# Layer-0 cross attention: which operand of the probabilities-times-context product is stationary

## The chip, the cores and the metric

The kernel runs on one core of a Trainium2 chip. The metric is device time in microseconds (us), from launch to end of one execution. Three timed runs of the kernel before gave 3319.53, 3310.01 and 3318.12 us, median 3318.12. The profile is of a further execution. Its span, from first to last instruction, is 3369.6 us, 1.6% above that median; profiling makes it longer. A difference read in the profile is therefore multiplied by 3318/3370 = 0.985 before it is set against the runs.

## The reference, cut to what matters

A two-layer Perceiver block on 128 sequences of 32 tokens with 256 features. Each sequence has its own context of 257 rows with 256 features. The part that is changed is the first residual term:

```
x = x + L0_xattn(layernorm(x), ctx)
q = x1 @ Wq + bq ; k = ctx @ Wk + bk ; v = ctx @ Wv + bv
attn = softmax(q k^T / sqrt(256))           # 32 x 257 for each sequence, one head
out  = attn @ v                             # 32 x 256
```

Then follow self attention (16 heads), a quantised feed-forward network (FFN), cross attention with 16 heads on the same context (layer 1), self attention, and a mixture of experts. Everything is computed in float32 or in pairs of float16 numbers. Since the rows of attn sum to one, out = (attn @ ctx) @ Wv + bv. The kernel uses that: it forms attn @ ctx (called a1) and multiplies it by Wv afterwards.

## The kernel before, in words

A tile is four sequences, 128 tokens on 128 partitions; there are 32 tiles. Three parts run after each other: the first (layer-0 attention, self attention, FFN and the layer-1 cross attention), the second, and the third (experts). This change touches the first part and the seam to the second.

The first part runs two lanes, each with its own buffers and its own four banks of PSUM (`ps[:, 0..3]`). A tile is split in a first half of steps (`tensor1`, `scalar1`, `vector1`: from the norm of x to the FFN's two up products) and a second half (`tensor2`, `scalar2`, `vector2`: the FFN's last product and the layer-1 cross attention). While one lane is in the second half of its tile (the older lane, `o`), the other is in the first half of the next tile (the younger, `y`). One such overlay is called a half period here; there are 31 of them in the first part, and the younger lane's product a1 stands in each once. Together with the first tile, which runs alone, that makes 32 products.

Each engine is an in-order queue. In which order an engine takes the steps of both lanes is written out by hand as a string of `o` and `y` in `ORDER["first"]` (one string for each engine, and one for SyncE, which issues the loads). `ORDER["between"]` holds the same for the seam, which runs once. A wait in one step holds up everything behind it on that engine. Steps announce their end on a semaphore that `did(name)` counts, and `need(name)` waits for it. `STEPS` lists the names for each engine.

The steps around the change, in the younger lane: `s1_ps` (scores of four sequences, each on its own 32 columns of TensorE), `exps1` (exponential on ScalarE), `pt1_ps` (three transposes, L557), `pt1_f` (ScalarE copies them to SBUF as `pt1`), `a1_ps` (L565 and L569), `a1_f` (ScalarE copy to `op`), `y1_ps` (times Wv, L401), and `x_1` (VectorE adds the result to x, L923), followed by the next norm (`xn2`, L892) and its transposes (`xt_ps2`, L528).

The product a1 is formed turned, features on partitions and tokens on columns, as `y1_ps` needs it. For each of the two halves of the features there is one 128x128 product for the last context row of each sequence (L565: context stationary), and eight products for four sequences by two groups of 128 context rows (L569). In each of these the context (128 rows x 128 features) is the stationary operand and 32 columns of turned probabilities are the moving one. A float32 product shows in the trace as two MATMUL records with a weight load each.

The older lane meanwhile forms values (`v4_ps`, L381, 128x256), the last value row (`vl_ps`, L651, one 32-column group of TensorE for each sequence), and keys (`k4_ps`, L381, 128x257). VectorE copies the keys (`k4_f`, L1004) and ScalarE copies `vl` four times with a scale (`vl_f`, L843). Then come eight score products (`s4_ps`, L682) and eight rounds of turned scores (`st4_ps`, L711 and L715) and values (`o4_ps`, L732 and L735). Between the rounds VectorE takes a reciprocal (L1014) and multiplies (L1015, `om4`), which frees the bank for the turned scores two rounds on. At the end are `sel` (L1020), `y4_ps` (L781) and `x_4` (L1024). The half period ends when VectorE has the quantised activations `hq` (L984) and TensorE turns them (`hq_ps`, L742).

Of the kernel before, what the change touches and what calls it, by code (L numbers as in the profile page):

```python
# [13 lines left out]
P = 128  # L14
D = 256
C = D // P
SEQ = 32
SEQS = 128
KEYS = 257
NB = P // SEQ  # L20
# [79 lines left out]
def each(names, n):  # L100
# [3 lines left out]

STEPS = {
    "xattn": dict(
        tensor="xt_ps1 q0_ps qbk_ps s1_ps pt1_ps a1_ps y1_ps".split(),
        scalar="xt1_f q0_hi q0_hi exps1 pt1_f a1_f".split(),
        vector="ln_var1 xn1 q0_lo q0_lo exp_bias1 p1_last x_1".split(),
        gpsimd="ln_rstd1 biased1".split()),  # L110
    "selfattn": dict(
        tensor="xt_ps2 qk_ps v_ps self_s self_pt o2_ps self_y".split(),
        scalar="xt2_f qe_act v2_f self_p pt2_f sel2_act sel2_act".split(),
        vector="ln_var2 xn2 qk_f qe self_shift p2_norm sel2 sel2".split(),
        gpsimd="ln_rstd2 biased2".split()),
    "ffn": dict(
        tensor="xq_ps gate_ps gate_ps up_ps up_ps".split(),
# [5 lines left out]
        scalar=["hqt"]),  # L123
# [35 lines left out]
for _stage, _engines in STEPS.items():  # L159
    for _engine, _names in _engines.items():  # L160
# [12 lines left out]

ORDER = {
    "first": dict(
        tensor=("oyoyoyyooooyooyoyooooyoyooyooooyoooyoyooyooooooyyooyyooyoo"),
        scalar=("oyyyoooyoyooooooyooyoooyyoyooyoyyoooooyoyyooo"),
        vector=("yyyyoyoooooyyoyyyoyyooooyyoyyyoyoooyooooyooyyyyyooyyooyyyyoyoyyyooyyyyooyyooyyooyooyoyyyyyo"),
        gpsimd=("yoyyoooyoyo"),
        sync=("yyyyyyyyooo"),  # L180
    ),
    "between": dict(
        tensor=("oooyooooooooooooooooooooooyooyyooyyyyooyyooyoooooo"),
        scalar=("oooooooooooooooooyyyooyoyooyoooyyoyyoyoyoyy"),
        vector=("oyyyyyooooooooooooooooooooooyyoyoyooyoyoyyoyoyyyyooooyooooooyy"),
        gpsimd=("yoooooo"),
        sync=("ooo"),
    ),
# [54 lines left out]
def carve(memory, at, words, dt=F32):  # L243
    a = memory[:, at:at + words]
    return a if dt == F32 else a.bitcast(dt)


def build(nc, x_in, ctx_t, ctx_n, ctx_l, weights, ffn, experts, expert_b, consts, biases, rows, mid, sorted_rows, pair_rows, out):
    ctx = ExitStack()
    with ctx:  # L250
# [47 lines left out]
        def w1(name, k, n):  # L298

            a = W1_AT + W_AT[0][name]  # L300
            return mem[:, a:a + k * n].rearrange("p (k n) -> p k n", k=k)
# [96 lines left out]
        def by_token(pe, dst, weight, act, k=C):  # L398

            for kc in range(k):  # L400
                last = pe.matmul(dst, act[:, kc], weight[:, kc], start=(kc == 0), stop=(kc == k - 1))  # L401
            return last


        def first_half(lane):
# [15 lines left out]

            probs = carve(arena, 2048, KEYS)
            pt1 = carve(arena, 2308, 384)

            qe = carve(arena, 0, 512).rearrange("p (c b e q) -> p c b e q", c=C, b=NB, e=2)
            s2 = carve(arena, 512, 512)
# [106 lines left out]
            def tensor1(pe, t):  # L533
                def need(name, n=1):
                    pe.wait_ge(*at(t, name, n))
# [24 lines left out]
                need("pt1_f")  # L560
                pe.wait_ge(s[f"l_in{lane}"], total(t, 16, 16))
                pe.wait_ge(s[f"n_in{lane}"], total(t, 64, 64))
                for c in range(C):
                    cols = slice(c * P, (c + 1) * P)
                    pe.matmul(ps[:, 2, cols], ctx_lf[:, cols], pt1[:, 256:384], start=True, stop=False)  # L565
                    for b in range(NB):
                        for m in range(2):
                            toks = slice(m * P + SEQ * b, m * P + SEQ * (b + 1))
                            last = pe.matmul(ps[:, 2, c * P + SEQ * b:c * P + SEQ * (b + 1)], ctx_nf[:, b, m, cols], pt1[:, toks],  # L569
                                             start=False, stop=(b == NB - 1 and m == 1))  # L570
                last.then_inc(*did("a1_ps"))
                yield
                need("a1_f")
                by_token(pe, ps[:, 3, 0:D], w1("v0", C, D), op).then_inc(*did("y1_ps"))
                yield

# [22 lines left out]
                    last = pe.transpose(ps[:, 1, g * P:(g + 1) * P], s2[:, g * P:(g + 1) * P], ident)  # L599
                last.then_inc(*did("self_pt"))  # L600
                yield
                need("v2_f")
                need("pt2_f")
                pe.sem_inc(s["pe_goes"], 1)
                for c in range(C):
# [179 lines left out]
            def act_copy(act, t, dst, src, done, ready, n=1):  # L785

                act.wait_ge(*at(t, ready, n))
                act.activation(dst, src, ACT.Copy).then_inc(*did(done))  # L788
                yield

            def scalar1(act, t):
                yield from act_copy(act, t, xt[:, :, :].rearrange("p c n -> p (c n)"), ps[:, 0, 0:D], "xt1_f", "xt_ps1")
                act.wait_ge(*at(t, "q0_ps"))
                for c in range(C):
                    act.activation(q0[:, 0, c], ps[:, 1, c * P:(c + 1) * P], ACT.Identity, bias=qk_bias[:, c:c + 1]).then_inc(*did("q0_hi"))
                    yield
                act.wait_ge(*at(t, "exp_bias1"))
                act.activation(probs, ps[:, 0, 0:KEYS], ACT.Exp, bias=small[:, 3:4], accum_out=small[:, 4:5]).then_inc(*did("exps1"))
                yield
                yield from act_copy(act, t, pt1, ps[:, 1, 0:384], "pt1_f", "pt1_ps")  # L800
                yield from act_copy(act, t, op[:, :, :].rearrange("p c n -> p (c n)"), ps[:, 2, 0:D], "a1_f", "a1_ps")

                yield from act_copy(act, t, xt[:, :, :].rearrange("p c n -> p (c n)"), ps[:, 0, 0:D], "xt2_f", "xt_ps2")
                act.wait_ge(*at(t, "qk_f"))
                act.activation(qe[:, :, :, 0, :], qk_f[:, 0:2].rearrange("p c (b q) -> p c b q", b=NB), ACT.Copy, scale=parity[:, 0:1]).then_inc(*did("qe_act"))
                yield
                yield from act_copy(act, t, v2, ps[:, 0, 0:D], "v2_f", "v_ps")
                act.wait_ge(*at(t, "self_shift"))
                act.activation(s2, s2, ACT.Exp, scale=16 ** -0.5).then_inc(*did("self_p"))
                yield  # L810
                yield from act_copy(act, t, pt2.rearrange("p g n -> p (g n)"), ps[:, 1, :], "pt2_f", "self_pt")
                act.wait_ge(*at(t, "o2_ps"))
                for c in range(C):
                    act.activation(op[:, c].rearrange("p (b q) -> p b q", b=NB), ps[:, :, 64 * c:64 * c + SEQ], ACT.Identity,
                                   scale=parity[:, 0:1], bias=bcol("bv0")[:, c:c + 1]).then_inc(*did("sel2_act"))
                    yield

                yield from act_copy(act, t, xqt.rearrange("p c n -> p (c n)"), ps[:, 3, 0:P].bitcast(BF16), "xqt", "xq_ps")
                act.wait_ge(*at(t, "gate_ps", 1))
                act.activation(th3[:, 0:512], ps[:, 0, :], ACT.Tanh, scale=small[:, 11:12]).then_inc(*did("tanh"))  # L820
                yield
                act.wait_ge(*at(t, "gate_ps", 2))
                act.activation(th3[:, 512:1024], ps[:, 1, :], ACT.Tanh, scale=small[:, 11:12]).then_inc(*did("tanh"))
                yield
# [1116 lines left out]
```

## Time and profile before

| What | Value |
|---|---|
| median of three runs | 3318.12 us |
| span of the profiled execution | 3369.6 us |
| TensorE matmul (PE) busy | 2701.8 us, 80% |
| TensorE weight loads (PEld) busy | 2102.4 us, 62% |
| VectorE (DVE) busy | 1869.2 us, 55% |
| ScalarE (ACT) busy | 1046.4 us, 31% |
| GpSimd (POOL) busy | 495.2 us, 15% |
| mean granted TensorE clock | 0.913 |

Start with the shares of busy time, then look at the first part alone (62 to 2042 us), and there at one half period in order of time. Busy times of matmuls are modelled and overlap each other in latency. The distance between the starts of neighbouring rows is what a step costs TensorE, not the duration in the row. Granted clock 1.00 is 2.4 GHz and 0.50 is 1.2 GHz; a fraction between them is a mean over both.

### The profile page before, as it was taken

The numbers are of one execution on the slowest core, as the hardware profiler recorded it, in microseconds if no ns is written. First come the engines' busy times: TensorE is split into PE (matmuls) and PEld (weight loads), VectorE is DVE, ScalarE is ACT, GpSimd is POOL, SyncE is SP. The second block draws the span as 40 slices with busy tenths as digits, with TensorE's granted clock in tenths as the row PEclk, the third lists the DMA queues.
The fourth block names the chain that finished last, engine by engine and source line by source line (L and its number), as shares of the span: only waits on it lengthen the run. The fifth ranks groups of instructions, "written<-read, shape, count | busy, mean of one in ns | idle before, by whom it ended". The sixth has DMA issues, their size and how long they took to land.

```text
span 3369.6 us, 114292 instructions
## 1 busy us (share of the span) xinstructions
PE 2701.8 (80%) x45688; PEld 2102.4 (62%) x45783; DVE 1869.2 (55%) x5000; ACT 1046.4 (31%) x2120; POOL 495.2 (15%) x616
## 2 busy tenths in 40 slices
PE   3788888888888888888888887787788888858882
PEld 3566666676676676676676675566666666646662
DVE  4555556655655655655655655555555555545555
ACT  1333333333333333333333333222222222212220
POOL 2111111111111111111111111011111111112221
PEclk9889989988998998998999998899999999979996
DMA  5011111111111111111111112200000000021225
GB/s 176 22 38 50 30 38 51 30 41 48 31 43 44 32 42 44 32 43 44 32 43 43 33 45 72 96 14 17 14 14 14 16 14 14 14 73 62 69 66 178
DMA packets 86140, 153.57 MB, mean 46 GB/s; under 512 B 11224, under 2 KB 39904, under 8 KB 84576
## 3 DMA queue, kind: packets, MB, share of 16 engines
q1 hardware_dynamic: 73136, 117.78, 11.5%
q0 software_dynamic: 6528, 17.87, 1.4%
q10 hardware_dynamic: 6192, 13.38, 1.1%
q8 instruction: 270, 4.42, 0.5%
q14 instruction: 14, 0.11, 0.0%
HBM read 120.37 MB, written 28.62 MB: 44 GB/s over the span
## 4 chain that ended last, share of the span: by engine, by line
issue 54%; PE 24%; DVE 8%; POOL 6%; ACT 3%; DMA 2%; DVEq 2%; SPq 0%; POOLq 0%; ACTq 0%
PE ps L381 15%; POOL mem L463 3%; PE ps L1164 2%; PE ps L1479 2%; POOL x L1036 2%; PE ps L1116 1%; POOL rstd L1030 1%; DVEq L1457 1%; DVE mem L1348 1%; DVE mem L1527 1%; DMA y_tok<-mem 1%; DVE mem L1322 1%; DVE mem L1378 1%; DVE mem L1379 1%; DVE mem L1382 1%
## 5 line engine op out<-in xcount | busy, mean ns | idle before, releaser
L381 PE MATMUL ps<-mem 128*128 128x256 f16 (+1 forms) x4224 | 566.2, 293 | 76.1 <-DVE mem L1348 66.9
L381 PEld LDWEIGHTS ps<-mem 128*128 128x128 f16 x4224 | 439.2, 106 | 168.4 <-DVE mem L1348 70.4
L788 ACT ACTIVATE mem<-ps 128x512 f32<-128x512 f32 (+3 forms) x320 | 177.5, 565 | 430.6 <-PE ps L742 135.1
L381 PE MATMUL ps<-xt,mem 128*128 128x128 f16 x4608 | 280.4, 220 | 30.0 <-DVE xt L1303 30.0
L381 PEld LDWEIGHTS ps<-xt,mem 128*128 128x128 f16 x4608 | 261.4, 98 | 40.4 <-DVE xt L1303 37.4
L1030 POOL TENSOR_TENSOR rstd<-var_eps,neg_half 128x1 f32<-128x1 f32 x128 | 70.4, 550 | 1210.8 <-DVE var_eps L889 1210.8
L463 POOL TENSOR_TENSOR mem<-mem 128x514 f16<-128x514 f32 x136 | 161.1, 1187 | 569.2 <-ACT mem L458 569.2
L1004 DVE COPY mem<-ps 128x514 f32<-128x514 f32 x128 | 88.9, 694 | 262.8 <-PE ps L381 262.8
L1014 DVE RECIPROCAL mem<-ps 128x64 f32<-128x64 f32 x256 | 142.6, 557 | 161.9 <-PE ps L735 160.3
L832 ACT ACTIVATE mem<-ps 128x512 f32<-128x512 f32 x256 | 152.3, 595 | 174.9 <-PE ps L715 174.5
L715 PE MATMUL ps<-mem 64*128 64x128 f32 x2048 | 201.1, 319 | 0.0
L715 PEld LDWEIGHTS ps<-mem 64*128 64x128 f32 x2048 | 148.8, 205 | 63.0 <-issue 63.0
L1479 PE MATMUL ps<-mem 128*128 x576 | 155.9, 394 | 35.1 <-ACT mem L1505 34.3
L711 PE MATMUL ps<-ident,neg_max 128*128 128x256 f16 x512 | 110.0, 300 | 68.3 <-DVE mem L1015 60.9
L1009 DVE TENSOR_REDUCE neg_max<-ps 128x2 f16<-128x514 f32 x256 | 161.3, 682 | 0.0
L1479 PEld LDWEIGHTS ps<-mem 128*128 128x128 f32 x576 | 98.9, 191 | 71.1 <-issue 63.2
L732 PE MATMUL ps<-mem,ones 128*32 128x64 f32 x4096 | 137.0, 219 | 3.6 <-issue 3.1
L732 PE MATMUL ps<-mem 128*32 128x64 f32 x4096 | 139.2, 225 | 0.0
L1423 POOL DMA_INDIRECT x_sorted<-mem,pair_u x64 | 64.2, 1002 | 482.6 <-DVE pair_u L1394 472.8
L388 PE MATMUL ps<-xt,mem 128*128 128x128 f32 x768 | 122.6, 320 | 0.9 <-ACT xt L788 0.9
L569 PE MATMUL ps<-mem 128*128 128x32 f32 x1024 | 122.9, 275 | 0.0
L569 PEld LDWEIGHTS ps<-mem 128*128 128x128 f32 x1024 | 122.8, 196 | 0.0
(256 smaller groups left out, 5056.9 us busy)
## 6 DMA issues: line engine op xcount, KB each, us to landing
mem<-in_ctx_t SPq DMA_DIRECT2D x136, 257.0 KB, 2.8
mem<-in_ctx_n SPq DMA_DIRECT2D x136, 256.0 KB, 3.3
mem<-x_sorted SPq DMA_DIRECT2D x74, 128.5 KB
mem<-y_pairs SPq DMA_DIRECT2D x32, 256.0 KB, 4.1
mem<-in_experts ACTq DMA_DIRECT2D x7, 768.0 KB, 9.1
x<-in_x_tok SPq DMA_DIRECT2D x34, 128.0 KB, 3.5
x_mid<-x SPq DMA_DIRECT2D x32, 128.0 KB, 1.8
x<-x_mid SPq DMA_DIRECT2D x32, 128.0 KB, 2.0
```

The costliest lines, as they stand in the source:

```text
L381: last = pe.matmul(dst, a, b, start=i == 0 and j == 0, stop=i == n - 1 and j == 2)
L388: last = pe.matmul(dst[:, i * P:(i + 1) * P], weight[:, kc, oc * P:(oc + 1) * P], act[:, kc], start=(kc == 0), stop=(kc == 1))
L463: pool.tensor_tensor(ctx_tp[:, 1, :, b, :], stage_t[:, b % 2, :].rearrange("p (c m) -> p c m", c=C), ctx_tp[:, 0, :, b, :], ALU.subtract). ...
L569: last = pe.matmul(ps[:, 2, c * P + SEQ * b:c * P + SEQ * (b + 1)], ctx_nf[:, b, m, cols], pt1[:, toks], start=False, stop=(b == NB - 1 an ...
L711: pe.matmul(ps[:, 2 * c + i, 0:2 * P], neg_max[:, 2 * b + c, i:i + 1].to_broadcast([P, P]), ident16[:, :].unsqueeze(1).to_broadcast([P, 2, ...
L715: last = pe.matmul(ps[:, 2 * c + i, m * P:(m + 1) * P], kp[64 * i:64 * i + 64, c, b, m * P:(m + 1) * P], queries(c, b, i), start=False, st ...
L732: last = pe.matmul(dst, ones[:, 0:SEQ] if one else vp[:, b, m, feats], pt4[:, c, i, m, part], start=(m == 0 and not one), stop=False)
L788: act.activation(dst, src, ACT.Copy).then_inc(*did(done))
L832: act.activation(pt4[:, c].rearrange("p i m n -> p i (m n)"), ps[:, 2 * c:2 * c + 2, 0:2 * P], ACT.Exp, scale=64.0).then_inc(*did("p4"))
L1009: dve.tensor_reduce(neg_max[:, u, :], ps[:, 2 * c:2 * c + 2, 0:KEYS], X, ALU.max, negate=True).then_inc(*did("s4_max"))
L1014: yield from then(dve.reciprocal(recip[:, c], ps[:, 2 * c, 320:384]))
L1479: last = pe.matmul(ps[:, bank, 0:D], xt7[:, kc], mem[:, bass.ds(at_w + (EXPERTS_AT + 2 * D * kc + cols), D)], start=(kc == 0), stop=(kc == 1))
```

## The change

The roles of the operands are exchanged. The turned probabilities of one sequence (128 context rows x 32 tokens) become stationary, on that sequence's own group of 32 TensorE columns, and the context rows (256 features wide) move. That makes eight products instead of sixteen, and one 128x256 product for the last rows instead of two of 128x128. The result now has tokens on partitions. ScalarE copies it to a new buffer `a1`, TensorE transposes it in two pieces (`at1_ps`, into bank 1), and ScalarE copies it to `op` (`at1_f`). Then `y1_ps` is as before. One wait that another one covers (`v2_f` ahead of `o2_ps`) is dropped. The strings of `ORDER["first"]` and `ORDER["between"]` are written anew for all engines.

```diff
-        tensor="xt_ps1 q0_ps qbk_ps s1_ps pt1_ps a1_ps y1_ps".split(),
-        scalar="xt1_f q0_hi q0_hi exps1 pt1_f a1_f".split(),
+        tensor="xt_ps1 q0_ps qbk_ps s1_ps pt1_ps a1_ps at1_ps y1_ps".split(),
+        scalar="xt1_f q0_hi q0_hi exps1 pt1_f a1_f at1_f".split(),
@@ ORDER["first"]
-        tensor=("oyoyoyyooooyooyoyooooyoyooyooooyoooyoyooyooooooyyooyyooyoo"),
-        scalar=("oyyyoooyoyooooooyooyoooyyoyooyoyyoooooyoyyooo"),
-        vector=("yyyyoyoooooyyoyyyoyyooooyyoyyyoyoooyooooyooyyyyyooyyooyyyyoyoyyyooyyyyooyyooyyooyooyoyyyyyo"),
-        gpsimd=("yoyyoooyoyo"),
-        sync=("yyyyyyyyooo"),
+        tensor=("ooyoyyoooyooyoyoyoyooyooyooooyooyoooyoyooyooooyyooyyooyoooo"),
+        scalar=("oyyooyoyooyooooyyooyoooooyyoyooyyyoooyooyyoooo"),
+        vector=("oyyyyyooooooyyyooyyooyooyyyyyyoyoooyooooyooyyyyyooyyooyyyyyooyyyyyyyyooooyyyooyyyoyooyoyoyo"),
+        gpsimd=("yyooyyooyoo"),
+        sync=("yoyyyyyyyoo"),
@@ ORDER["between"]
-        tensor=("oooyooooooooooooooooooooooyooyyooyyyyooyyooyoooooo"),
-        scalar=("oooooooooooooooooyyyooyoyooyoooyyoyyoyoyoyy"),
-        vector=("oyyyyyooooooooooooooooooooooyyoyoyooyoyoyyoyoyyyyooooyooooooyy"),
+        tensor=("oooyooooooyoooooyooyoyooyooyyooooyooyooyoooooooooo"),
+        scalar=("oyyooooyooooooooooyoyoyoooyooyoyyoyoyyoyooo"),
+        vector=("yoyyyoooooyoyooyyoooooyooyooooyoooyyooyyoyyoyooooyooyooyoooooo"),
@@ first_half
+            a1 = carve(arena, 2692, D)
@@ tensor1
+                for m in range(2):
+                    for b in range(NB):
+                        pe.matmul(ps[SEQ * b:SEQ * (b + 1), 2, 0:D], pt1[:, m * P + SEQ * b:m * P + SEQ * (b + 1)], ctx_nf[:, b, m, :], start=(m == 0), stop=False)
+                pe.matmul(ps[:, 2, 0:D], pt1[:, 256:384], ctx_lf, start=False, stop=True).then_inc(*did("a1_ps"))
+                yield
+                need("a1_f")
                 for c in range(C):
-                    cols = slice(c * P, (c + 1) * P)
-                    pe.matmul(ps[:, 2, cols], ctx_lf[:, cols], pt1[:, 256:384], start=True, stop=False)
-                    for b in range(NB):
-                        for m in range(2):
-                            toks = slice(m * P + SEQ * b, m * P + SEQ * (b + 1))
-                            last = pe.matmul(ps[:, 2, c * P + SEQ * b:c * P + SEQ * (b + 1)], ctx_nf[:, b, m, cols], pt1[:, toks],
-                                             start=False, stop=(b == NB - 1 and m == 1))
-                last.then_inc(*did("a1_ps"))
-                yield
-                need("a1_f")
+                    last = pe.transpose(ps[:, 1, c * P:(c + 1) * P], a1[:, c * P:(c + 1) * P], ident)
+                last.then_inc(*did("at1_ps"))
+                yield
+                need("at1_f")
                 by_token(pe, ps[:, 3, 0:D], w1("v0", C, D), op).then_inc(*did("y1_ps"))
@@ tensor1, ahead of o2_ps
-                need("v2_f")
@@ scalar1
-                yield from act_copy(act, t, op[:, :, :].rearrange("p c n -> p (c n)"), ps[:, 2, 0:D], "a1_f", "a1_ps")
+                yield from act_copy(act, t, a1, ps[:, 2, 0:D], "a1_f", "a1_ps")
+                yield from act_copy(act, t, op[:, :, :].rearrange("p c n -> p (c n)"), ps[:, 1, 0:D], "at1_f", "at1_ps")
```

Read as steps, the new orders differ in these places. TensorE goes `vl a1 k4 at1 k4 y1 k4 k4 xt2 s4 s4 qk` where it went `vl a1 k4 y1 k4 k4 k4 s4 xt2 s4 qk`. It goes `hq ffn_y xt1 v4 q0` where it went `hq xt1 ffn_y q0 v4`. The FFN's transposes `xq_ps` stand behind the fourth `o4`, where they stood behind the fifth. ScalarE copies the fourth `v4` ahead of `pt1_f` instead of behind it. It takes `l4_exp` ahead of `self_p`, and `at1_f` stands ahead of `q4_h` and of all `k4_h`. VectorE finishes `rq3`, `sel`, `hq`, `x_4` in that order at the end of the half period. It takes the third key copy ahead of `xn2` and behind `x_1` and the norm's statistics, and the fourth behind `xn2`.

## Rows read from the trace of the kernel before

**Rows 1.** Page: busy times, group of L569; last row: L569's source view.

```profile
PE 2701.8 (80%) x45688; PEld 2102.4 (62%) x45783; DVE 1869.2 (55%) x5000; ACT 1046.4 (31%) x2120; POOL 495.2 (15%) x616
...
L569 PE MATMUL ps<-mem 128*128 128x32 f32 x1024 | 122.9, 275 | 0.0
...
L569 PE MATMUL ps<-mem x1024: 195/276/401, 65.4 to 2017.4; 128*128 128x32 f32 x171
```

**Rows 2.** Windows: stretch, length, busy us by engine, granted clock, DMA share, GB/s.

```profile
62.00:2042.00 1980.00, 1678.50 (x28567) 1292.09 (x28659) 1128.20 (x2825) 727.62 (x1430) 273.84 (x342) 0.91 0.13 40
2042.00:2110.00 68.00, 51.99 (x1032) 38.51 (x1034) 39.21 (x82) 25.74 (x39) 7.93 (x10) 0.90 0.21 76
```

**Rows 3.** Waits of PE, 100 to 2040 us: total us, times, longest.

```profile
PE ps L781 <- DVE mem L1020: 74.6, 30, 2.5
PE ps L711 <- DVE mem L1015: 57.7, 67, 0.9
```

**Rows 4.** Timeline of PE around one a1: start, us, operation, count, [idle before].

```profile
1062.93 0.38 PE L557 MATMUL ps<-cst,mem 128*128 128x128 f32 x2
...
1063.25 1.47 PE L381 MATMUL ps<-mem 128*128 128x256 f16 x12
1064.66 0.84 PE L651 MATMUL ps<-mem 128*32 128x256 f16 x24
1065.43 0.49 PE L565 MATMUL ps<-mem 128*128 128x128 f32 x2
...
1069.47 1.48 PE L381 MATMUL ps<-mem 128*128 128x257 f16 x12
1070.79 1.03 PE L401 MATMUL ps<-mem,op 128*128 128x256 f32 x4
1071.65 4.14 PE L381 MATMUL ps<-mem 128*128 128x257 f16 x36
...
1075.94 0.44 PE L528 MATMUL ps<-cst,xn 128*128 128x128 f32 x2
1076.59 0.28 PE L682 MATMUL ps<-mem 64*128 64x257 f16 x2 [0.20 <-DVE mem L1004]
```

**Rows 5.** Timeline of PE, float32 products on four column groups.

```profile
1107.43 0.29 PE L732 MATMUL ps<-mem,ones 128*32 128x64 f32 x8
1107.54 0.29 PE L732 MATMUL ps<-mem 128*32 128x64 f32 x8
```

**Rows 6.** Timeline of ACT ahead of and beside the same a1.

```profile
1063.13 0.98 ACT L788 ACTIVATE mem<-ps 128x512 f32<-128x512 f32 x2 [1.15 <-PE ps L381]
...
1064.76 0.60 ACT L788 ACTIVATE mem<-ps 128x512 f32<-128x512 f32 x1 [0.66 <-PE ps L381]
1065.55 1.57 ACT L843 ACTIVATE mem<-ps,quad 128x256 f32<-128x256 f32 x4 [0.19 <-PE ps L651]
```

**Rows 7.** Timeline of DVE behind the same a1.

```profile
1072.03 0.48 DVE L923 SCALAR_TENSOR_TENSOR x<-ps,small,x 128x256 f32<-128x256 f32 x1 [0.34 <-PE ps L401]
...
1075.12 0.52 DVE L892 TENSOR_SCALAR xn<-x,mv,rstd 128x256 f32<-128x256 f32 x1
1075.84 0.69 DVE L1004 COPY mem<-ps 128x514 f32<-128x514 f32 x1 [0.20 <-PE ps L381]
```

**Rows 8.** Timeline, the self attention's probabilities and their transposes.

```profile
1087.56 0.69 DVE L947 TENSOR_TENSOR mem<-mem,small 128x512 f32<-128x512 f32 x1
...
1089.30 1.11 PE L599 MATMUL ps<-cst,mem 128*128 128x128 f32 x4
```

**Rows 9.** Timeline of PE at the end of the half period.

```profile
1112.01 1.13 PE L781 MATMUL ps<-mem 128*128 128x256 f32 x4 [2.49 <-DVE mem L1020]
1114.10 0.82 PE L742 MATMUL ps<-identb,mem 128*128 128x128 bf16 x8 [0.96 <-DVE mem L984]
```

**Rows 10.** Windows: two stretches of that half period; columns as in rows 2.

```profile
1091.00:1114.00 23.00, 16.58 (x495) 11.71 (x486) 16.43 (x43) 8.02 (x16) 2.77 (x3) 1.00 0.01 4
1114.40:1121.20 6.80, 5.47 (x29) 4.34 (x27) 2.57 (x12) 2.04 (x4) 1.64 (x3) 0.50 0.30 97
```

More of the change, by code:

```diff
@@ L562, in tensor1 @@
                 pe.wait_ge(s[f"n_in{lane}"], total(t, 64, 64))
-                for c in range(C):
-                    cols = slice(c * P, (c + 1) * P)
-                    pe.matmul(ps[:, 2, cols], ctx_lf[:, cols], pt1[:, 256:384], start=True, stop=False)
+                for m in range(2):
                     for b in range(NB):
-                        for m in range(2):
-                            toks = slice(m * P + SEQ * b, m * P + SEQ * (b + 1))
-                            last = pe.matmul(ps[:, 2, c * P + SEQ * b:c * P + SEQ * (b + 1)], ctx_nf[:, b, m, cols], pt1[:, toks],
-                                             start=False, stop=(b == NB - 1 and m == 1))
-                last.then_inc(*did("a1_ps"))
+                        pe.matmul(ps[SEQ * b:SEQ * (b + 1), 2, 0:D], pt1[:, m * P + SEQ * b:m * P + SEQ * (b + 1)], ctx_nf[:, b, m, :], start=(m == 0), stop=False)
+                pe.matmul(ps[:, 2, 0:D], pt1[:, 256:384], ctx_lf, start=False, stop=True).then_inc(*did("a1_ps"))
                 yield
                 need("a1_f")
+                for c in range(C):
+                    last = pe.transpose(ps[:, 1, c * P:(c + 1) * P], a1[:, c * P:(c + 1) * P], ident)
+                last.then_inc(*did("at1_ps"))
+                yield
+                need("at1_f")
                 by_token(pe, ps[:, 3, 0:D], w1("v0", C, D), op).then_inc(*did("y1_ps"))
```

## The prediction

> **What bounds the kernel now.** I read the busy shares first, then the first part alone, then who PE waited for, and last one half period in order of time. PE is busy for 80% of the span and the next engine for 55% [rows 1]. In the first part PE is busy for 1678.5 of 1980 us and VectorE for 1128 [rows 2]. So there PE is the bound wherever it does not wait. Its waits lie in two places. At the end of each half period it stands about 2.5 us for `sel`. Between the rounds of turned scores and values it stands up to 0.9 us for a VectorE multiply [rows 3]. Around the product a1 there is no wait at all: from 1062.93 to 1075.94 each row of PE starts where the one before it stops issuing [rows 4]. The costliest-group row says the same of L569, with 122.9 us busy and 0.0 idle before it [rows 1]. Time taken off PE there moves everything behind it forward, as long as the other engines follow.
>
> **What is removed.** Distances between starts count, not durations. The old a1 runs from 1065.43 to 1069.47, which is 4.04 us [rows 4], and PE is at full clock. These are 36 records (two for each of 18 products), 0.112 us each, though most move only 32 columns: they pay for weight loads and not for the product.
>
> **What is added on PE.** (1) Eight float32 products of 128x256, on four column groups. One float32 product of 256 columns on the whole array takes 0.43 us: two of them from 1070.79 to 1071.65 [rows 4]. If four column groups run at once, eight take 2 x 0.43 = 0.86 us; if they don't, 3.44 us. The trace of before has no float32 product of this width on column groups, so these are the two ends. Two rows are near it. Four float32 products of 64 columns on four groups pass in 0.11 us [rows 5]. The same four in turn would take 4 x 0.43 / 4 = 0.43, so four run at once, and 256 columns at that pace give 0.44 us for four. And 24 float16 products of 256 columns on column groups take 0.77 us, where 12 on the whole array take about 1.31, that is 0.109 each [rows 4]: 6 x 0.109 = 0.65 would be perfect overlap, so 0.12 is lost. I take 0.88 plus 0.12. (2) The last rows: one product of 0.43. (3) Two float32 transposes: three of them go from 1062.93 to 1063.25, so 0.11 each, 0.22 in all [rows 4]. Sum 1.65 us. PE saves 4.04 - 1.65 = 2.39 us in each tile.
>
> The 0.12 us bears on a rule of the Trainium skill, TensorEngine Tiling (Array Packing), section Tiling Modes: changing the tiling mode, unlike changing the tile, drains TensorE. That speaks against a change that adds such switches. By the row above, whatever a switch and back costs is within the 0.12 us, so the rule alone can't take more than a twentieth of the saving.
>
> **What is added elsewhere.** ScalarE gets one copy of 128x256 more. It is busy for 37% of the first part [rows 2], and k4 number 2 on PE (1.31 us) covers the copy after the transposes. The copy ahead of them is covered by k4 number 1. The new buffer and the removed wait cost nothing: ScalarE makes `v2_f` before `pt2_f`, for which PE waits anyway.
>
> **What is late next.** Four waits take part of the saving back.
> - a1 waits for `pt1_f`. The fourth v4 copy now stands ahead of it on ScalarE. Counted from the end of that v4 on PE, ScalarE needs 0.1 + 0.60 for the copy and 0.38 to 0.49 for `pt1_f` (two copies in 0.98 [rows 6]), plus some 0.1 of signals: 1.3. PE has three transposes (0.32) and vl (0.77) in between, 1.09. Wait 0.2.
> - The first keys need all four `vl_f`: 1.57 us for four [rows 6]. They start when `pt1_f` ends, and a1 fills only 1.43 of that. Wait 0.2. Before, 4.04 us of a1 hid it.
> - `xt_ps2` needs `xn2`. From the start of `x_1` to the end of `xn2` before is 1072.03 to 1075.64 with a key copy in between [rows 7]. Without that copy (0.69) it is about 2.9 from the end of y1. PE now has two k4 there (2.62), not three. With the fourth key copy behind `xn2` the second score product waits again. I set 0.5 for both, against 0.4 now, of which the row shows 0.20 [rows 4]: 0.1 more.
> - The self attention's exponential now stands behind `l4_exp`, some 0.8 us later. Its probabilities are ready at 1088.25 and PE takes them at 1089.30 [rows 8], so here it is hidden. Other half periods may have less to spare; between 0 and 0.8, I take 0.2.
>
> Together 0.7; net gain 2.39 - 0.7 = 1.7 us per tile.
>
> **The new orders elsewhere.** At the end of the half period I followed VectorE's new sequence step by step with the old durations. The FFN's transposes come one round (2.8 us) earlier, PE waits there for VectorE, and the last `o4` ends about 0.5 us later than now. But then `sel` and `hq` follow each other without a gap, and y4 fills the wait before `hq_ps`. `hq_ps` comes at the same place: now it is 1114.10 after waits of 2.49 and 0.96 [rows 9]. At the head, `ffn_y` before `xt1` exchanges one wait for another. I take zero for both, with -1 to +1 us per half period as bounds, since all of the 3.45 us of these two waits could be neither saved nor doubled by a change of order in which VectorE does the same work. The seam runs once: PE is idle for 16 of 68 us [rows 2], the bound is 8 us either way, I take zero. SyncE now holds the younger lane's loads behind one of the older lane. They are needed a half period later at the earliest, and DMA is busy for 13% [rows 2], so zero.
>
> **Sum.** 32 x 1.7 = 54 us of a span of 3369.6. Times 3318/3370 that is 53 us: 3318 - 53 = 3265 us. The bounds of the terms: the net of a tile lies between 0.7 and 2.7 (waits doubled and an end effect of -1 at half weight; no waits and a small end gain), which gives 3296 to 3233.
>
> **Rivals.**
>
> A. The clock comes back (more gain). Behind the tail's waits PE runs at the lower clock (1.2 GHz): the stretch from 1114.40 to 1121.20 holds 5.47 us of PE work at 0.50 [rows 10]; at 2.4 GHz that is half. If the denser tail (y4 right before `hq_ps`) keeps the clock up there, 2.7 us more are gained: 31 x 2.7 = 84, in all 3318 - 53 - 82 = 3183. For it: y4 now lies next to `hq_ps`. Against it: PE still stands some 3 us for `sel` before y4.
>
> B. The saving becomes a wait (no change). PE reaches the score products earlier, but what comes there is VectorE's: x_1, the norm, two key copies, eight maxima. If the added copy, the transposes and the order leave this chain as late as now, a tile gains 0.3 or less, 3308 to 3320; I name 3312. For it: the chain a1, copy, transposes, copy, y1 now has two more hand-overs, and xn2 is awaited already. Against it: that chain gets shorter by 4.04 - 1.43 on PE and longer by about 0.22 and 0.6. The Trainium skill, TensorEngine Tiling (Array Packing), section PSUM Bottleneck, warns of this: after a fourfold speed-up on TensorE the copy out of PSUM may become the bottleneck. By it the time would be this rival's; ScalarE's 37% speaks against it.
>
> C. A clock loss among the rounds (slower). The stretch from 1091 to 1114 runs at 1.00 now, with PE busy for 16.6 of 23 us [rows 10]. With the FFN's transposes one round earlier, PE meets a wait of 0.8 for VectorE and 0.6 for ScalarE right behind the round that has no filler, and the fifth exponential stands behind that copy. If the granted clock falls to 0.50 there for a stretch as long as those at the other places, 6.8 us, the PE work in it, 0.72 of the time, is done at half speed: 0.5 x 0.72 x 6.8 = 2.45 us lost per half period, net 1.7 - 2.45 = -0.75, times 31 = 23: 3341. It decides from 4.7 us of low clock per half period. For it: the low stretch at the tail lies behind just such gaps, of 2.49 and 0.96 [rows 9]. Against it: the gaps there are no larger in sum than today's.
>
> D. The column groups don't overlap at 256 float32 columns (slower). Then a1 takes 3.44 + 0.43 + 0.22 + 0.12 = 4.2, and the waits for `pt1_f`, xn2 and the probabilities stay: 0.2 + 0.5 = 0.7 lost, 32 x 0.7 = 22: 3340. Rows 5 speak plainly against it.
>
> **Chances.** Forecast 0.57, A 0.13, B 0.12, C 0.12, D 0.06. About 0.3%, 10 us, is what a measurement of this kernel can tell from no change. The forecast's own range, 3233 to 3296, is all faster, and so is A, and a third of B. Faster 0.74, same 0.08, slower 0.18. For 8 in 10 the range goes down into the way to A and up to B's end: 3195 to 3318; C and D (0.18) and the last of A are left out.
>
> **What would show it.** a1's rows on PE span about 1.4 us, with eight 128*32 products in about 0.9 (against D). The keys behind it start with an idle of about 0.2 for L843 (the vl wait). `xt_ps2` starts about 1.7 us earlier, counted from the start of a1. The mean half period, now (2017.4 - 65.4) / 31 = 63 us from one a1 to the next [rows 1], becomes 61.3. PE's total wait for `sel` stays near 75 to 95 us, and the stretches at low clock keep their number and place. I am wrong if L569's successor takes over 3 us, if the low stretches move into the rounds or vanish at the tail, or if the half period stays at 63.

## The result, and the profile after

Four runs of the changed kernel gave a median of 3238.47 us (3232.08 to 3243.41), against 3318.41 before. That is 80 us less. The ratio of the runs is 0.9751, 95% interval 0.9736 to 0.9767, so 2.5% faster. The forecast was 3265 with a range of 3195 to 3318. The number lies well inside, but that is partly luck. The experiments below show that two terms of the forecast were too small, and that a loss which it did not look for took most of the difference away again.

The page of the changed kernel begins so (busy us, share, instructions; the row of q8 has packets, MB and share of the DMA engines):

```profile
span 3230.2 us, 113315 instructions
...
PE 2529.7 (78%) x45176; PEld 1939.6 (60%) x45271; DVE 1856.3 (57%) x5000; ACT 1044.1 (32%) x2152; POOL 495.3 (15%) x616
...
q8 instruction: 397, 6.50, 0.8%
```

The kernel before had 270 packets on that last queue, which fetches instructions. The forecast never looked at it. The windows of the profile (length, busy us by engine, granted clock, DMA share, GB/s) split the program at the first and the last `hq_ps`. The first stretch is the first part, the second is the second part with its seam.

Changed kernel:

```profile
106.00:1897.50 1791.50, 1501.39 (x28210) 1126.27 (x28304) 1105.43 (x2820) 724.66 (x1457) 273.18 (x341) 0.97 0.14 43
1897.50:2871.30 973.80, 745.51 (x15551) 603.89 (x15549) 515.79 (x1522) 226.78 (x451) 128.83 (x167) 0.87 0.09 32
```

The kernel before, profiled once more (span 3322.0 us):

```profile
108.50:2058.70 1950.20, 1684.42 (x28799) 1282.94 (x28799) 1125.93 (x2821) 726.10 (x1426) 273.38 (x341) 0.91 0.13 39
2058.70:2963.30 904.60, 734.39 (x15550) 595.94 (x15550) 521.54 (x1522) 227.09 (x451) 127.67 (x168) 0.91 0.09 32
```

The first part became 159 us shorter, three times what was forecast. The second part, in which the diff changes only the order at the seam, became 69 us longer.

The first profile of before, 3369.6 us, was a long execution. Its first part is as long as here (1952.0 us), its second part 948.5 us. The execution of this second profile took 3323.88 us for a span of 3322.0, among timed runs with a median of 3321.83. So profiling did not make it longer, and the factor of 0.985 in the forecast was an error, worth 1 us there.

Around a1 the changed kernel's PE goes so (start, us, operation, count, [idle before]), to be held against [rows 4]:

```profile
295.96 0.84 PE L651 MATMUL ps<-mem 128*32 128x256 f16 x24
296.94 1.07 PE L566 MATMUL ps<-mem 128*32 128x256 f32 x16
297.94 0.70 PE L567 MATMUL ps<-mem 128*128 128x256 f32 x2
298.55 1.49 PE L381 MATMUL ps<-mem 128*128 128x257 f16 x12
299.88 0.38 PE L571 MATMUL ps<-cst,mem 128*128 128x128 f32 x2
300.09 1.49 PE L381 MATMUL ps<-mem 128*128 128x257 f16 x12
301.42 1.03 PE L401 MATMUL ps<-mem,op 128*128 128x256 f32 x4
302.29 2.81 PE L381 MATMUL ps<-mem 128*128 128x257 f16 x24
305.17 0.44 PE L529 MATMUL ps<-cst,xn 128*128 128x128 f32 x2
```

And ScalarE beside it ([rows 6]):

```profile
295.74 0.98 ACT L788 ACTIVATE mem<-ps 128x512 f32<-128x512 f32 x2 [0.71 <-PE ps L381]
296.85 1.57 ACT L844 ACTIVATE mem<-ps,quad 128x256 f32<-128x256 f32 x4
```

The eight products on column groups (L566, 16 records) take 1.00 us from start to start, as forecast (0.88 + 0.12). The two transposes take 0.21. The vl products cost 0.77 and a1 starts 0.98 after them, so the wait for `pt1_f` is 0.2. L567 ought to take 0.43 and the keys start 0.61 after it, 0.1 after the fourth `vl_f` ends (296.85 + 1.57 = 298.42): that wait is 0.2 too. The transposes of x start 2.88 us after the start of two keys that take 2.62.

At the end of the half period ([rows 9]):

```profile
339.52 1.13 PE L781 MATMUL ps<-mem 128*128 128x256 f32 x4 [2.04 <-DVE mem L1021]
340.50 0.62 PE L742 MATMUL ps<-identb,mem 128*128 128x128 bf16 x8
342.23 1.05 PE L748 MATMUL ps<-mem 128*128 128x256 bf16 x8 [1.11 <-ACT mem L788]
```

The wait ahead of `hq_ps` (0.96) is gone and the one ahead of y4 is 0.45 shorter. `ffn_y` (L748) takes 1.05 us here, at the full clock (window 340.4 to 345: 1.00). In the second stretch of [rows 10] the clock was 0.50, and the same eight products took 1.70 us from start to start:

```profile
1116.73 1.91 PE L748 MATMUL ps<-mem 128*128 128x256 bf16 x8
1118.43 1.92 PE L388 MATMUL ps<-xt,mem 128*128 128x128 f32 x8
```

Not every half period looks like this one. Counted in the granted clock of the trace, between the two bounds of the first part, it was at 0.50 for 340 us before (second profile) and for 102 us in the changed kernel. Before, it fell at all 31 ends of a half period, and again in most, 26 times some 33 us later and 6 times some 19 us later. In the changed kernel it fell at 18 ends and nowhere else.

### The profile page after: what moved, and what is told of

It reads as the page before. It is cut to its first block, busy times and chain, and to the rows that moved or that the text cites. A ratio compares the mean times of both kernels' runs of the same rounds, so it can differ in the third digit from the quotient of the medians.

```text
span 3230.2 us, 113315 instructions
## 1 busy us (share of the span) xinstructions
PE 2529.7 (78%) x45176; PEld 1939.6 (60%) x45271; DVE 1856.3 (57%) x5000; ACT 1044.1 (32%) x2152; POOL 495.3 (15%) x616
## 4 chain that ended last, share of the span: by engine, by line
PE 58%; DVE 21%; issue 10%; ACT 6%; DVEq 2%; DMA 2%; SPq 0%; ACTq 0%; POOL 0%; POOLq 0%
PE ps L381 25%; PE ps L401 3%; PE ps L388 3%; DVE mem L1015 3%; PE ps L732 2%; PE ps L1480 2%; PE ps L1165 2%; PE ps L715 2%; ACT mem L788 1%; PE ps L781 1%; DVE mem L974 1%; PE ps L748 1%; DVE neg_max L1010 1%; PE ps L1117 1%; DVE small L979 1%
## 5 line engine op out<-in xcount | busy, mean ns | idle before, releaser
L381 PE MATMUL ps<-mem 128*128 128x256 f16 (+1 forms) x4224 | 580.7, 298 | 89.2 <-DVE mem L1349 81.4
L788 ACT ACTIVATE mem<-ps 128x512 f32<-128x512 f32 (+4 forms) x352 | 185.8, 547 | 376.8 <-PE ps L620 126.1
L715 PE MATMUL ps<-mem 64*128 64x128 f32 x2048 | 183.2, 298 | 0.0
L715 PEld LDWEIGHTS ps<-mem 64*128 64x128 f32 x2048 | 134.3, 187 | 53.9 <-issue 53.9
L711 PE MATMUL ps<-ident,neg_max 128*128 128x256 f16 x512 | 100.1, 277 | 56.9 <-DVE mem L1016 52.8
L1480 PEld LDWEIGHTS ps<-mem 128*128 128x128 f32 x576 | 99.7, 193 | 69.6 <-issue 61.5
L1199 ACT ACTIVATE xt<-ps 128x256 f16<-128x256 f32 x64 | 24.5, 383 | 306.5 <-PE ps L1097 306.5
L1165 PE MATMUL ps<-mem 32*64 32x32 f32 x4096 | 61.8, 249 | 66.4 <-issue 65.0
L1323 DVE TENSOR_TENSOR mem<-ps,bias 128x512 f32<-128x512 f32 x128 | 88.2, 689 | 44.1 <-PE ps L1117 24.9
```

The lines of the kernel that those rows point to most:

```text
L381: last = pe.matmul(dst, a, b, start=i == 0 and j == 0, stop=i == n - 1 and j == 2)
L711: pe.matmul(ps[:, 2 * c + i, 0:2 * P], neg_max[:, 2 * b + c, i:i + 1].to_broadcast([P, P]), ident16[:, :].unsqueeze(1).to_broadcast([P, 2, ...
L715: last = pe.matmul(ps[:, 2 * c + i, m * P:(m + 1) * P], kp[64 * i:64 * i + 64, c, b, m * P:(m + 1) * P], queries(c, b, i), start=False, st ...
L1165: last = pe.matmul(ps[64 * hh:64 * hh + 64, b, SEQ * j:SEQ * (j + 1)], v5[keys, j * P + 64 * hh:j * P + 64 * hh + 64], pt5[keys, j // 2, S ...
L1480: last = pe.matmul(ps[:, bank, 0:D], xt7[:, kc], mem[:, bass.ds(at_w + (EXPERTS_AT + 2 * D * kc + cols), D)], start=(kc == 0), stop=(kc == 1))
```

## The experiments

Eleven runs follow, with the short names (e1, e2 and so on) that the expectations and the text use. The diffs leave out repeated lines, and a string cut short is marked by dots. "Not busy" below is the length of a window less PE's busy time in it.

### The kernel before, profiled again

Run e1. No edit. 

> The kernel before, unchanged, profiled once more. The two profiles differ by 139 us (3369.6 to 3230.2), the runs by 80. If the first profile of before was a long execution, this span is near 3316, and the mean half period of the first part is well under 62.97 us (about 61.3, if all 53 us lie there). If the profile is always longer than the runs for this kernel, the span is again near 3370 with 63 us per half period.

3321.83 us; ratio 0.9996, interval 0.9982 to 1.0009. The span was 3322.0, but the expectation for the half period failed: it is 62.9 us again, and 44 of the 48 us of difference lie in the second part. The first profile has 48.5 us of waits for nothing known ahead of L1164 there, in 121 pieces, and the second profile has 2.1 us. 270 packets were fetched in both. Why the first execution had these waits stays open.

### The product alone, with the old orders

Run e2.

```diff
 ORDER["first"] of before, with the two new steps
-        tensor=("oyoyoyyooooyooyoyooooyo...
-        scalar=("oyyyoooyoyooooooyooyooo...
+        tensor=("oyoyoyyooooyooyoyoyoooyo...
+        scalar=("oyyyoooyoyooooooyyooyooo...
```

> The new product, its two transposes and the second copy, with the old orders (the new steps put in behind a1: TensorE goes a1, k4, at1, k4, y1, k4, k4, and ScalarE a1_f, at1_f). Theory P: TensorE bounds this place, and the time taken off it is the gain; 2.4 us less in 32 tiles, some 0.5 lost to waits: 60 us, 3258. Rival O: the new orders bring most of the 80 us; then this is 3290 or more.

3329.21 us; ratio 1.0013, interval 0.9991 to 1.0035: no change that shows. Theory P seemed dead. But the windows say that both parts of the program moved:

```profile
105.60:1993.50 1887.90, 1572.26 (x28303) 1155.51 (x28303) 1130.48 (x2820) 732.53 (x1457) 273.72 (x341) 0.94 0.14 41
1993.50:2974.30 980.80, 758.52 (x15551) 609.58 (x15550) 514.73 (x1522) 227.18 (x451) 127.49 (x168) 0.86 0.09 31
```

Against e1 the first part is 62 us shorter, and the second 76 us longer with the same instructions. This kernel also fetched 397 packets of instructions.

### The orders alone, with the old product

Run e3. Of the new strings only TensorE's is shown.

```diff
 ORDER["first"] and ORDER["between"] of the changed kernel, without the at1 steps
+        tensor=("ooyoyyoooyooyoyooyooyooyooooyooyoooyoyooyooooyyooyyooyoooo"),
```

> The old product with the new orders (without the steps of the new transposes), in the first part and at the seam. Theory P with an order that only moves waits: 3300 to 3320. Rival O: 3250 to 3270. If both parts count, e2 and e3 add up to about 80.

3249.38 us; ratio 0.9778, interval 0.9751 to 0.9805: 72 us faster, as rival O said (just under its range). There were 270 packets. The first part:

```profile
108.10:1980.20 1872.10, 1599.28 (x28799) 1227.87 (x28800) 1105.11 (x2820) 717.03 (x1426) 273.43 (x341) 0.96 0.13 41
```

It is 78 us shorter than in e1. PE is not busy for 273 us of it (266 in e1), so its waits are no shorter in sum. Its busy time fell by 85 us for the same instructions, at a granted clock of 0.96 instead of 0.91.

### The kernel before, kept busy in its waits

Run e4.

```diff
+                keep_busy(pe, ps[:, 3, 384:512], ident16[:, :], 34)
                 need("sel")
                 ... y4 ...
+                keep_busy(pe, ps[:, 3, 384:512], ident16[:, :], 12)
@@ tensor1
+                keep_busy(pe, ps[:, 3, 384:512], ident16[:, :], 18)
                 yield from transpose_x(pe, t, 1)
```

> The kernel before, with 64 small products of float16 (128x128, results unused) in the three waits of TensorE at the end of each half period: 34 ahead of y4, 12 behind it, 18 ahead of the transposes of x, 56 ns each at full clock, 3.6 of the 4.8 us that TensorE stands there. Theory C: part of the gain of the changed kernel is clock (low stretches of the first part went from 341 to 109 us between the profiles); then keeping TensorE busy removes the low stretch behind the tail and brings 31 x 1.5 to 2.5 us: 3240 to 3275. If the clock there brings nothing, the time is 3318 or a little above.

3282.00 us; ratio 0.9879, interval 0.9856 to 0.9901: 39 us faster by adding work whose results nobody uses. The first part shows why, with more PE work and a higher clock:

```profile
109.00:2014.30 1905.30, 1721.12 (x30783) 1344.61 (x30783) 1133.70 (x2821) 724.08 (x1426) 273.52 (x341) 0.97 0.14 40
```

45 us are gained there, 1.45 in each of 31 half periods. That is a little under the 1.5 to 2.5 expected, and the time is 7 us above the expected range. The low clock is gone at the ends of the half periods (1 left of 31) and remains at other places, 122 us in all. So the waits at the end of a half period cost this kernel twice, once as time and once more as the lower clock behind them.

### The changed kernel, its TensorE program shifted

```diff
             pe.wait_ge(s["pool_set"], POOL_SETUP)
+            for _ in range(64):
+                pe.matmul(psum[:, 0, 0:P], ident16[:, :], ident16[:, :], start=True, stop=True)
             pe.wait_ge(s["ffn_abs"], 3)
```

Run e5. 

> The changed kernel with 64 float16 products (results unused) at the start of TensorE's program, where it waits for the setup. They make TensorE's program 128 instructions longer ahead of its loops, about as many as the new product took out of it. Theory F: in the kernels with the new product the loop of the second part no longer stays where its instructions are held, and is fetched again in every trip (397 packets of 16 KB on the instruction queue against 270, the 127 more all in the second part, and L1165 waits 65 us for nothing else); it depends on where the loop begins. Then here: 270 packets or so, the second part 905 us and not 974, and the time 3165 to 3180. Rival S: the second part is slower for another reason (the clock, the state the first part leaves); then 3238 again with 397 packets.

3157.74 us; ratio 0.9500, interval 0.9484 to 0.9516: another 81 us, from work that computes nothing, at the start of the program. That is 7 us under the range of theory F. The number of packets is 270 again:

```profile
q8 instruction: 270, 4.42, 0.6%
```

The second part shows what stood in the way. PE's waits there, in the changed kernel (total us, times, longest):

```profile
PE ps L381 <- DVE mem L1349: 81.4, 32, 8.1
PE ps L1165 <- issue: 65.0, 29, 3.4
```

And in the shifted one:

```profile
PE ps L381 <- DVE mem L1349: 88.8, 32, 8.1
...
PE ps L1165 <- issue: 2.0, 1, 2.0
```

"issue" means that the engine waited for nothing the profile knows. In the timeline of the changed kernel it sits at the same place in every trip, twice:

```profile
2304.90 1.48 PE L381 MATMUL ps<-mem 128*128 128x256 f16 x12
2308.55 0.56 PE L1165 MATMUL ps<-mem 32*64 32x32 f32 x31 [2.16 <-issue]
2311.52 1.62 PE L1165 MATMUL ps<-mem 32*64 32x32 f32 x97 [2.41 <-issue]
```

In the shifted kernel the same step runs through:

```profile
2303.38 1.48 PE L381 MATMUL ps<-mem 128*128 128x256 f16 x12
2304.79 1.82 PE L1165 MATMUL ps<-mem 32*64 32x32 f32 x128
```

The loop of the second part makes 15 trips. Over it the stall falls from 65.0 to 2.0 us, and the second part from 973.8 to 912.5:

```profile
105.20:1888.80 1783.60, 1510.77 (x28304) 1121.26 (x28305) 1105.69 (x2820) 725.28 (x1457) 273.37 (x341) 0.98 0.14 43
1888.80:2801.30 912.50, 736.29 (x15551) 597.37 (x15549) 522.52 (x1522) 226.86 (x451) 128.97 (x168) 0.91 0.09 32
```

The first part is 8 us shorter as well.

### The kernel before, shifted in the same way

Run e6. The same edit in the kernel before. 

> The kernel before with the same 64 products at the start. Theory F, if only the place within a 16 KB packet decides: the second part is fetched again in every trip as in the changed kernel, about 397 packets, 3380 to 3395. If the shift has no effect on the kernel before: 3320.

3386.63 us; ratio 1.0216, interval 1.0184 to 1.0248: 66 us slower. 397 packets, the second part 951.6 us, and the stall at the same line:

```profile
PE ps L1164 <- issue: 60.5, 27, 3.1
```

So it is neither the new product nor the 64 extra ones by themselves. What decides is how much of TensorE's program stands ahead of the second part's loop.

### The product alone, shifted

Run e9. The same edit in the kernel with the new product and the old orders. 

> e2 (new product, old orders) with the 64 products at the start. Theory F with theory P: the product gives its 60 us once the second part is no longer fetched again: 3255 to 3265. Rival S: 3329 as e2, and the product itself is worth nothing.

3256.34 us; ratio 0.9799, interval 0.9783 to 0.9816: 64 us, as theories F and P said together. There were 270 packets. First and second part:

```profile
105.70:1996.80 1891.10, 1566.13 (x28304) 1153.75 (x28305) 1130.15 (x2821) 731.76 (x1457) 273.37 (x341) 0.95 0.13 41
1996.80:2901.10 904.30, 735.79 (x15550) 596.63 (x15550) 522.10 (x1522) 227.08 (x451) 127.69 (x168) 0.91 0.09 32
```

### The changed kernel, shifted and kept busy

Run e8. The shift, and 32 products in `keep_busy` ahead of `need("sel")`.


> e5 with 32 more float16 products (results unused) ahead of y4 at the end of each half period, 1.8 of the 2.0 us that TensorE waits there. Theory C: the low stretch left behind the tail (2.8 us of the 3.3 per half period) goes, 31 x 1 us: 25 to 40 us under e5. If the clock brings no more: as e5.

3150.17 us; ratio 0.9477, interval 0.9461 to 0.9494. It is the fastest version, but its interval overlaps that of the shifted one, and the expected 25 to 40 us did not come. The granted clock of the first part did rise, from 0.98 to 0.99, while its length went from 1783.6 to 1786.3 us. This does not show that the last of the low clock is worth nothing. PE's waits for nothing known in the first part went up from 8 to 30 us, since the 32 products in each half period also make the program longer and move its code. They can have eaten the gain, and the two were not tried apart.

### Which of the new orders

Late orders (run e10): those of the changed kernel from the fourth turned scores on, the old ones before. Early orders (run e11): the other way round. Both have the old product and the old seam. Only some of the strings that change are shown.

```diff
 late
-        tensor=("...yooyooooooyyooyyooyoo"),
-        scalar=("...yoyyoooooyoyyooo"),
+        tensor=("...yooyooooyyooyyooyoooo"),
+        scalar=("...yoyyoooyooyyoooo"),
```

> The kernel before with the new orders only from the fourth turned scores on (FFN transposes one round earlier, sel, hq and x_4 one after the other at the end), the old ones up to there and at the seam. Of the 78 us that the new orders save in the first part, theory T says that this part brings most, since the waits at the end of the half period shrink (hq_ps from 0.96 to 0.2, y4 from 2.5 to 2.0) and with them the low stretch behind them: 3262 to 3280. Rival H: it is the head, and here it is 3300 or more. The forecast had zero for both.

3279.03 us; ratio 0.9855, interval 0.9826 to 0.9884: 49 us. The time is in the range of theory T, but the low clock did not go with the waits as it had said:

```profile
108.10:2008.70 1900.60, 1659.89 (x28799) 1274.55 (x28800) 1104.40 (x2820) 722.92 (x1426) 273.68 (x341) 0.92 0.13 40
```

PE is not busy for 241 us, 25 less than in e1, and its busy time is 24 us less. The clock still fell at 27 of the 31 ends of a half period.

> The complement: the new orders (ffn_y ahead of the transposes of x, the moved copies, exponentials, norm steps, loads and GpSimd's steps) up to the fourth turned scores, the old ones from there on. Theory T: 3295 to 3320. Rival H: 3260 to 3280, with the low stretch 30 to 40 us into the half period (3.7 us of each before) gone.

3332.88 us; ratio 1.0015, interval 1.0002 to 1.0029: no gain, 13 us above the range of theory T. The low clock some 33 us behind the ends is gone, which rival H had named as its sign. It fell at every end as before and 15 times some 19 us later. PE is not busy for 311 us, 45 more than in e1, and busy for 39 us less:

```profile
109.70:2065.80 1956.10, 1645.40 (x28800) 1250.01 (x28801) 1135.02 (x2821) 720.31 (x1426) 273.03 (x341) 0.93 0.13 39
```

PE's waits in the first part of this kernel (110 to 1880 us) hold two that are new:

```profile
PE ps L748 <- ACT mem L788: 32.4, 29, 1.1
PE ps L599 <- DVE mem L947: 30.0, 28, 1.1
```

The first of these took the place of the wait for xn ahead of L528 (34.2 us in the second profile of before, same stretch). The second is that for the self attention's probabilities behind `l4_exp`. The early and late parts together brought 72 us, so some 20 us come from having both, or from the seam, which was not tried alone.

### Half of the shift

Run e12. The changed kernel with 32 products at the start.


> The changed kernel with 32 instead of 64 products at the start of TensorE's program (64 instructions, 4 KB). If the loop of the second part is held whole whenever it touches one packet fewer, this is one or the other: 270 packets and 3158, or 397 and 3238. If the refetch grows with the misplacement, something between.

3191.47 us; ratio 0.9587, interval 0.9559 to 0.9615. There were 270 packets, and the second part took 905.6 us: for that part it is one or the other. But the time lies between the two, since the first part took 1818.1 us and not 1783.6. PE waited 15.8 us there for "issue" ahead of L609 (11 times), which in the fully shifted kernel is 0.2, and the granted clock was 0.96, not 0.98. So the place of the code costs time in the long loop of the first part too. Why it does with 32 products and not with 64 is open.

## Why the forecast came out right, point by point

| Kernel (run) | us | first part | PE busy in it | not busy | clock | second part | packets |
|---|---|---|---|---|---|---|---|
| before (e1) | 3318 to 3322 | 1950 | 1684 | 266 | 0.91 | 905 | 270 |
| before, shifted (e6) | 3387 | 1957 | 1667 | 289 | 0.92 | 952 | 397 |
| product (e2) | 3329 | 1888 | 1572 | 316 | 0.94 | 981 | 397 |
| product, shifted (e9) | 3256 | 1891 | 1566 | 325 | 0.95 | 904 | 270 |
| orders (e3) | 3249 | 1872 | 1599 | 273 | 0.96 | 909 | 270 |
| both (the change) | 3238 | 1792 | 1501 | 290 | 0.97 | 974 | 397 |
| both, shifted (e5) | 3158 | 1784 | 1511 | 273 | 0.98 | 912 | 270 |

The forecast added 53 us for the product, zero for the orders and nothing for the second part. Where the second part is not fetched again, the orders bring 72 us (before to e3) and the product another 92 on top (e3 to e5). The repeated fetch takes 81 back (e5 to the change). That makes 83, against the 80 measured. The terms that were too small and the loss that was not seen partly cancel, so the nearness of the number is luck.

**The product: terms of TensorE right, worth too small.** The two terms that the trace shows by themselves are as written: 1.00 us for the eight products, 0.21 for the transposes against 0.22. Rival D (no overlap of column groups) is false: 16 records in 1.00 us. The waits for `pt1_f` and `vl_f` are 0.2 each as written. That for the self attention's probabilities was taken as 0.2 and is 32.0 us in 30 half periods, 1.07 each. It comes with the orders and not with the product, since e3 has it too (31.0 us).

With the old orders the product alone brought 64 us (e9). But the sum was for the new orders. From e3 to e5 the first part gets 88.5 us shorter, all of it in PE's busy time, while the time not busy stays at 273 us. The work taken out is 31 x 2.39 = 74 us of that. The rest goes with the clock, 0.96 to 0.98, and was not measured by itself. So a half period gets 2.9 us shorter (60.4 to 57.5, from one a1 to the next) and not 1.7: the 0.7 us of waits set against the saving were not lost in sum. With the old orders they were, and more, 59 us in all (266 to 325), and a clock of 0.95 instead of 0.91 made up for much of it.

**The orders: this step failed.** The step "The new orders elsewhere", with its "I take zero for both", was wrong. The orders are worth 72 us, 49 of them with the late part alone. As a sum of PE's waits zero was nearly right, 266 us not busy before and 273 with the new orders. What was put at nothing is the clock. The forecast had it only in rival A, at 82 us and a chance of 0.13. In the trace PE does the same instructions in 85 us less, and the time at 0.50 in the first part goes from 340 to 133 us. e4 puts a price on the clock: 0.91 to 0.97 is worth 39 us even with useless work added. So the truth lies between the forecast and rival A. Neither part of the orders does it alone. The late part shortens waits by 25 us and leaves the low clock at 27 ends of a half period. The early part leaves it at every end, has 265 us of it instead of 340, and pays for that in waits. Together they leave it at 18 ends. Which of the moved steps do that is open.

A smaller error of the same step is that VectorE was walked with the old durations. `xq_f` was entered with 0.72 us, but the changed kernel's takes 0.35 (source views of before and after: min/median/max ns):

```profile
L965 DVE TENSOR_SCALAR mem<-xn,small x32: 353/718/725, 99.4 to 2048.1; 128x256 f32<-128x256 f32 x32
```

```profile
L966 DVE TENSOR_SCALAR mem<-xn,small x32: 352/353/356, 95.8 to 1883.3; 128x256 f32<-128x256 f32 x32
```

Before, it ran beside a GpSimd subtraction (L463, 1100.06 to 1101.19 in that half period, `xq_f` from 1100.62 to 1101.34). In the new order GpSimd's is over (324.75 to 325.85) when it starts at 326.88. The late orders alone keep GpSimd's string, the two do not meet, and it takes 0.35 as well. With the early orders alone they overlap for less (subtraction 409.37 to 410.50, `xq_f` 410.15 to 410.65), and it takes 0.50. In both cases of overlap `xq_f` ends 0.15 us after the subtraction. So it looks held up until GpSimd is done. What the shorter `xq_f` is worth was not tried alone.

**The second part: not seen.** No step of the forecast touched it, and no rival did. Its instructions were fetched again in every trip. That cost 81, 73 and 66 us in the three pairs of runs (the change and e5, e2 and e9, e6 and before), as much as the whole measured gain. The runs show it by the packets of the instruction queue: over the second part 147 in the changed kernel and 21 in e5, of 16 KB each (6.50 MB in 397 packets).

The Trainium skill, Runtime: NRT & Kernel Launch, section Instruction fetch mechanics, says that TensorE's instruction memory holds 128 KiB, that is 2048 instructions, as a first-in first-out store refilled in blocks of 16 KiB. The traces agree on the blocks; no run shows the size of the store by itself. The second part has 15550 matmul records and as many weight loads for 16 tile pairs, 1944 a pair. At the 64 bytes an instruction that follow from this page of the Trainium skill, that is an estimated 124 KB a trip, plus waits and branches. The changed kernel fetches 126 packets more than e5 in the second part, some 8 for each of the 15 trips, which is a loop of that size fetched whole. By that estimate the loop fits in eight blocks only if it begins near the start of a block, and touches a ninth otherwise.

This is an explanation and was not shown directly, but four placements fit it. The new product makes each of its four copies in TensorE's program shorter by 32 records, so everything behind moves by some 8 KB, half a block (changed: fetched again). 64 small products with their weight loads are 128 records and put it back (e5: held). The same 64 in the kernel before push it out by half a block (e6: fetched again). And 32 of them (e12) were enough to have it held.

The same section of the Trainium skill calls the cost of crossing a 16 KiB boundary mostly hidden. Here, at the loop's return, 2.16 and 2.41 us in a trip are not hidden.

**The forecast's own signs.** The eight products came in 1.00 us and the keys waited 0.2, as it said. The half period is (1853.1 - 64.8) / 31 = 57.7 us, not 61.3. `xt_ps2` starts 2.3 us earlier, not 1.7. PE's wait for `sel` is 61.3 us in 30 half periods, not 75 to 95. The low stretches did not keep their number (63 before, 18 now), which by its own words counts against the forecast.

**Rivals.** A is partly true, as said. B (the saving becomes a wait) was what e2 looked like from its time alone, and is false as a whole, though with the old orders 59 us did become waits. C (a low stretch among the rounds) is false: the window from 316 to 339 us of the changed kernel, which answers to the first of [rows 10], still has 1.00, and all 18 low stretches of its first part lie at the ends of half periods.

## What to carry to other kernels

Compare the packets of the instruction queue before and after every edit. Here TensorE's loop of the second part lost or regained over 4 us a trip when code ahead of it grew or shrank, and an edit was judged by what it did to its neighbour. Read a total by the parts of the program before believing or dropping a theory: e2's time said that the product is worth nothing, its windows said 60 us. Split each part once more, into busy and not busy: the orders left the sum of the waits as it was and still brought 72 us. And where TensorE's clock falls behind its waits, price a wait with what the clock does after it.

## What the runs showed of the hardware

- A loop of some 1944 TensorE records a trip was fetched again in every trip or not at all, depending on how much code stood ahead of it: 2.16 and 2.41 us of stall in a trip, 397 packets against 270.
- Half a shift had the full effect there (270 packets), but the first part took 34 us more than with the full shift.
- 64 useless float16 products in TensorE's waits of each half period made a kernel 39 us faster (granted clock of the first part 0.91 to 0.97). 32 in a kernel at 0.98 made no difference that shows, with 22 us more of unexplained waits beside them.
- The same instructions on TensorE took 1684 or 1599 us of busy time (granted clock 0.91 and 0.96) while the time not busy was 266 and 273 us.
- Float32 products of 256 columns on four column groups overlap nearly fully: eight in 1.00 us, against 0.43 for one on the whole array.
- The same VectorE instruction (128x256, float32, from and to SBUF) took 0.35 us, and 0.72 or 0.50 where it started while a GpSimd subtraction ran, ending 0.15 us after it both times.
